# Two cross-attention layers on one core: where four loads, two stores and a split projection stand in each slot

## What is computed

```python
# layer 0 (8 heads of 40; the context's last 4 tokens are "ca", the first 73 "enc")
hs     = mha(x @ Wq, enc @ Wk, enc @ Wv)
ca_q1  = einsum('btc,th->bch', ca, Wq_ca)[:, indices]    # queries from 192 channels
ca_hs1 = mha(ca_q1, x, x)                                # keys and values are x itself
ca_hs2 = mha(ca_hs1 @ Wq, ca @ Wk_ca, ca @ Wv_ca)        # only 4 keys
x      = (hs + ca_hs2) @ Wout + b_out + x
# layer 1 (20 heads of 16, 77 keys)
out    = mha(x @ Wq1, ctx @ Wk1, ctx @ Wv1) @ Wo + bo + x
```

## Time and profile before

| what | value |
|---|---|
| runs | 377.20, 387.36, 387.67 us (median 387.36) |
| the profiled execution | 382.48 us; its span in the profile 380.6 us |
| mean granted clock of PE | 0.93 |
| PE busy (share of the span) | 331.5 us (87%) |
| PE weight loads, DVE, ACT, POOL busy | 257.9, 197.9, 161.1, 120.9 us |
| chain that ended last, by engine | PE 57%, ACT 11%, DMA 10%, DVE 9%, issue 6%, SP's queue 5% |
| DMA | 56.11 MB in 54468 packets, mean 147 GB/s |

### The profile page before, as it was taken

The page is one execution under the profiler, slowest core; times in us unless marked ns, Lnnn a source line. Parts: engine busy times, 40 slices in busy tenths (PEclk is TensorE's granted clock), DMA queues, the critical chain, the costliest instruction groups (busy, mean ns, idle before and its releaser), DMA issues.

```text
span 380.6 us, 7973 instructions
## 1 busy us (share of the span) xinstructions
PE 331.5 (87%) x3044; PEld 257.9 (68%) x3044; DVE 197.9 (52%) x431; ACT 161.1 (42%) x343; POOL 120.9 (32%) x124
## 2 busy tenths in 40 slices
PE   4998966999987999799979998999799979887685
PEld 2777654677755777687668767777687768646653
DVE  4552116272771478257736775377257742623544
ACT  3541550408451846074607461754084507350050
POOL 5836140025140714062306231714081203122201
PEclk9996998999985999799989999999699989979898
DMA  8998924704277527752685378628742872216011
GB/s 249 285 344 258 217 85 120 187 2 129 71 199 141 174 73 208 172 168 80 172 207 166 85 195 184 177 87 212 185 143 72 222 188 79 71 42 154 10 43 41
DMA packets 54468, 56.11 MB, mean 147 GB/s; under 512 B 17680, under 2 KB 47472, under 8 KB 54432
## 3 DMA queue, kind: packets, MB, share of 16 engines
q1 hardware_dynamic: 54432, 55.61, 53.6%
HBM read 36.12 MB, written 19.10 MB: 145 GB/s over the span
## 4 chain that ended last, share of the span: by engine, by line
PE 57%; ACT 11%; DMA 10%; DVE 9%; issue 6%; SPq 5%; POOL 1%; POOLq 0%; DVEq 0%; ACTq 0%
ACT prob L785 8%; PE bank L629 5%; DVE negm L910 5%; PE bank L452 4%; DMA q_scratch<-q 4%; PE bank L731 3%; PE bank L749 3%; PE bank L453 3%; PE bank L454 3%; PE bank L655 3%; PE bank L482 3%; PE bank L719 3%; PE bank L684 2%; PE bank L465 2%; PE bank L765 2%
## 5 line engine op out<-in xcount | busy, mean ns | idle before, releaser
L785 ACT ACTIVATE prob<-bank 77x512 f32<-77x512 f32 (+1 forms) x96 | 41.2, 529 | 22.6 <-PE bank L527 22.5
L910 DVE TENSOR_REDUCE negm<-bank 128x5 f32<-128x385 f32 (+2 forms) x88 | 42.5, 550 | 12.9 <-PE bank L765 12.9
L1167 POOL TENSOR_TENSOR at0lo<-atu,at0hi 120x512 fp32r<-120x512 f32 x8 | 14.8, 1854 | 107.1 <-ACT at0hi L775 107.1
L869 ACT ACTIVATE prob<-bank 73x512 f32<-73x512 f32 x32 | 16.3, 591 | 73.1 <-PE bank L713 73.1
L1175 POOL TENSOR_TENSOR xlo<-x,xhi 128x256 fp32r<-128x256 f32 x16 | 11.5, 738 | 77.1 <-DVE xhi L1056 77.1
L910 DVE TENSOR_REDUCE negmc<-bank 128x2 f32<-128x512 f32 x48 | 29.4, 681 | 7.8 <-PE bank L537 7.8
L525 PE MATMUL bank<-q,kp 32*77 32x256 f32 x320 | 24.9, 391 | 6.2 <-ACT prob L785 3.9
L684 PE MATMUL bank<-at0hi,wo 120*128 120x256 f32 x48 | 17.7, 370 | 13.8 <-issue 13.8
L775 ACT ACTIVATE q<-bank 120x512 fp32r<-120x512 f32 (+3 forms) x32 | 15.7, 489 | 27.9 <-PE bank L456 27.3
L1104 POOL TENSOR_TENSOR cast<-ca,small 96x1536 fp32r<-96x1536 f32 x8 | 22.3, 2790 | 13.1 <-PE bank L719 12.8
L876 ACT ACTIVATE prob<-bank 128x512 f32<-128x512 f32 x48 | 25.4, 624 | 0.0
(11 more groups left out here) (174 smaller groups left out, 866.1 us busy)
## 6 DMA issues: line engine op xcount, KB each, us to landing
q_scratch<-q SPq DMA_DIRECT2D x16, 360.0 KB, 4.2
q0s<-q_scratch SPq DMA_DIRECT2D x8, 640.0 KB
xt<-in_xt SPq DMA_DIRECT2D x8, 384.0 KB, 4.5
...
xkeys<-in_xkeys SPq DMA_DIRECT2D x8, 352.0 KB, 5.0
...
```

What stands on the lines that cost most here:

```text
L785: nc.scalar.activation(p1[:, h:h + n, :].rearrange("p h q -> p (h q)"), ps_of("SC1", j, d)[0:KEYS1, 0:n * SQ], ACT.Exp, scale=SCALE1)\
L869: nc.scalar.activation(p0[:, 2 * j:2 * j + 2, :].rearrange("p h q -> p (h q)"), ps_of("SC0", j, b)[0:KEYS0, :], ACT.Exp, scale=SCALE0)\
L910: return nc.vector.tensor_reduce(out=out, in_=in_, axis=AX, op=ALU.max, negate=True)
```

## The change

Four edits, with no change to the arithmetic.

- **SP.** The load of wo's rows stands first in the slot, ahead of denc. The channel keys (xkeys) are loaded after the two q0s loads instead of before them. The store of the output stands behind rb1's loads. In slot 8 rb1 is spread before atu1 is loaded. The denc of batch 0 is gathered at the end of slot 0.
- **OUT in two jobs.** In slots 3 to 7 OUT 1 (8 matmuls, and its addition on DVE) stands between CS and SC1 8; OUT 0 stays after S2. In slots 8 and 9 M1 stands between OUT 0 and OUT 1.
- **Setup.** V1 0-3 move ahead of CS in slot 1; CA stands ahead of V0 4-7 in slot 0. DVE's recc and atu0 of slot 1 stand behind the maxima.
- **Drain.** In slot 8 S2 and its exp stand ahead of all three PV1.

```diff
         if s4 and not s1:
-            jobs(e, "OUT", 0, 1)
+            jobs(e, "OUT", 0)
...
         if s3:
             jobs(d, "M1")
+        if s4 and not s1:
+            jobs(e, "OUT", 1)
...
+        if i == 1:
+            jobs(0, "V1", 0, 1, 2, 3)
...
             jobs(b, "CS", *range(6))
+        if s4 and s1:
+            jobs(e, "OUT", 1)
...
         if i == 0:
-            jobs(0, "V0", *range(3, B))
+            jobs(0, "V0", 3)
             jobs(0, "CA", 0, 1)
+            jobs(0, "V0", *range(4, B))
         if i == 1:
-            jobs(0, "V1", *range(B))
+            jobs(0, "V1", 4, 5, 6, 7)
+        if s2 and not s1:
+            jobs(c, "S2")
         if s3 and d < LAST:
-            jobs(d, "PV1", *(range(3) if s4 and s1 else range(1)))
+            jobs(d, "PV1", *(range(3) if s4 else range(1)))
...
-        if s2:
+        if s2 and s1:
             jobs(c, "S2")
         if s4 and s1:
-            jobs(e, "OUT", 0, 1)
-        elif s3 and d < LAST:
+            jobs(e, "OUT", 0)
+        elif s3 and not s4:
             jobs(d, "PV1", 1, 2)
...
                 if s2:
-                    drained(sp, "CU", c, 0, 1)
-                    sp.dma_start(denc[:, :], uc[D0:128:64, :, :]).then_inc(denc_in, 16)
+                    if c == 0:
+                        sp.wait_ge(v2w_st, 32)
+                    sp.dma_start(wo0[96:128, :, 2, :].bitcast(f32), v_d[c]).then_inc(v2w_in, 16)
+                    if c:
+                        gather_channel(c)
                     sp.wait_ge(recc_ready, c + 1)
...
                 if s1:
-                    if b:
-                        load_xkeys(b)
                     sp.wait_ge(q_st, 32 * (b + 1))
...
-                if s2:
-                    if c == 0:
-                        sp.wait_ge(v2w_st, 32)
-                    sp.dma_start(wo0[96:128, :, 2, :].bitcast(f32), v_d[c]).then_inc(v2w_in, 16)
+                    if b:
+                        load_xkeys(b)
...
-                if s4:
-                    store_out(e)
                 if s3 and d < LAST:
...
+                    if s1:
+                        load_rows1()
+                        spread_reciprocals1()
+                    else:
+                        spread_reciprocals1()
+                        load_rows1()
+                if s4:
+                    store_out(e)
...
+                    if b == 0:
+                        gather_channel(0)
...
                 if s4 and not s1:
-                    layer1_out(f)
-                if s2:
-                    dve.wait_ge(denc_in, 16 * (c + 1))
-                    nc.vector.reciprocal(recc[:, :], denc[:, :]).then_inc(recc_ready, 1)
...
+                    layer1_out(0)
+                if i > 1 and s2:
+                    channel_reciprocals()
+                if s4 and not s1:
+                    layer1_out(1)
+                if i > 1 and s2:
+                    layer0_rows()
                 if s1:
                     ca_maxima(*range(6))
+                if s4 and s1:
+                    layer1_out(1)
...
+                if i == 1:
+                    channel_reciprocals()
+                    layer0_rows()
                 if s2:
                     dve.wait_ge(rbc_in, 32 * (c + 1))
...
                 if s4 and s1:
-                    layer1_out(f)
+                    layer1_out(0)
```

138 lines of the change are left out of this document (81 added, 57 removed).

## The result

The changed kernel is **not faster, and in the first measurement slower**: 394.6 us in the median of 4 runs (387.8 to 398.3) against 385.1 for the kernel before (377.2 to 387.7), a ratio of 1.025 (95% interval 1.015 to 1.034). Run again later, it took 388.5 us (383.5 to 393.9, 4 runs) against 386.2, with no interval. A ratio in this text is taken over the runs within 1.5% of the fastest of their kernel, which are two of the four of the changed kernel each time, so it can stand up to 1% off the quotient of the medians. In the repetition these two (383.5 and 385.4) are level with the mean of the ten of the kernel before (384.6). So the kernel is between level and 2.5% slower, and whether it is slower by 2% is not settled. The forecast of 372 us and its range of 361 to 384 are missed by both medians, and no gain of any size was seen. The profiled executions took 392.3 and 383.5 us.

The account below looks back on a forecast made before the run. PE, busy 331.5 of 380.6 us, was taken as the bound, with SP's queue loop limiting the gain. From 382.5 us, -9.6 - 0.5 + 1 + 0 - 1.1 = -10.2 gave 372; own range 367 to 378, with two rivals 361 to 384.

Parts of the forecast that it names:

- wo first: Loading wo's rows first in the slot removes PE's stall ahead of O and its clock fall; 23.4 us at stake.
- A: Leg of SP's slot turn from line 424 to the load of q0s: 15.36 us in slot 3, to stay 15.4.
- C: Leg of SP's slot turn from rec1's start to the next line 424: 14.40 us in slot 3, to become 11.2.
- DVE path of 11.1 us: From rec1's start through rb1, the product, at1hi and rec0 to SP: 11.1 us, tying with C's 11.2.
- B: Leg of SP's slot turn from the load of q0s to rec1's start: 9.08 us in slot 3, to become 10.1.
- xkeys, "1.0" a slot: Loading xkeys behind q0s lengthens B by 1.0 us a slot, bounds -0.4 and 5.0.
- Rival 3: Slower (chance 0.08): xkeys ahead of the maxima and den1 cost B 5.0 us instead of 1.0; 395 to 400 us.
- The output store, "0.42 us of SP": Storing the output behind rb1 costs 0.42 us of SP ahead of xt and den0, within C.
- OUT in two, "0": OUT 1 moves to where PE waits for ACT's exps: 0, or -0.5 to +0.5 us a slot if PE decides.
- Setup, "0"; the bounds -1.5 and +1.5: Slots 0 and 1: V1's gain ahead of S2 is lost again behind late recc; 0 us, bounds -1.5 and +1.5.
- Drain, "-1.1": Slots 8 and 9: rb1 first and output last save about 0.8 us, M1 0.3 to 0.9; together -1.1 us.
- The two new waits, "+1, at most +8": PE waits at SC0 (about 1 us) and CU 1 (about 1.7); charged +1 us for all slots, at most +8.

Follow-up runs that it names:

- k0s early: W with k0s of the next batch loaded right behind xkeys instead of behind xt: 369.9 us, ratio 0.968.
- den0 early: W with the gather of den0 issued in front of xt and k0s instead of behind them: 386.7 us, ratio 1.007.
- W: The kernel before with wo's load first in the slot and OUT in two jobs, nothing else: 371.5 us (ratio 0.962), repeated 372.4 us (0.979).
- W + keys late: W with xkeys loaded behind q0s: 381.2 us, ratio 0.990.
- W with the whole setup: W with the setup work reordered as in the change: 379.4 us, ratio 0.984.
- recc early: W with the change's setup order, but slot 1's reciprocal of denc and product on atu0 ahead of the maxima: 365.1 us, ratio 0.950.
- W + drain: W with slots 8 and 9 reordered as in the change: 377.9 us, ratio 0.980.

## Why the prediction was wrong, step by step

**wo first: right in kind.** A stayed (15.0 against 15.4), O's stall went, and with it the fall of the clock there. Alone it gave 11.4 us in slots 2 to 7. By my terms it should have given more: -9.6 for six slots had 6 x 1.0 us for the keys already taken off. What is missing is in C.

**C, the step that failed.** I wrote that "both of SP's waits go: 14.40 - 3.1 - 0.5 + 0.4 = 11.2". It is 13.5 in slots 2 to 6, and 12.5 even with wo first alone. The waits did go; the leg did not get shorter by them. SP's timeline at the end of slot 3, before and changed (start us, us, queue, line, what):

```profile
164.02 0.34 SPq L303 DMA_DIRECT2D xt<-in_xt  x1
164.40 0.43 SPq L309 DMA_DIRECT2D k0s<-k_scratch  x1
164.87 0.45 SPq L311 DMA_DIRECT2D k0s<-k0lo_scratch  x1
168.50 0.55 SPq L414 DMA_DIRECT2D den<-u  x1
169.10 0.48 SPq L415 DMA_DIRECT2D u_scratch<-u  x1
169.62 0.42 SPq L416 DMA_DIRECT2D u0b_scratch<-u  x1
170.80 0.32 SPq L418 DMA_DIRECT2D rec_scratch<-rec  x1
```

```profile
166.47 0.34 SPq L416 DMA_DIRECT2D rec_scratch<-rec  x1
...
171.37 0.40 SPq L376 DMA_DIRECT2D out_t<-x  x1
171.88 0.36 SPq L312 DMA_DIRECT2D xt<-in_xt  x1
172.29 0.47 SPq L318 DMA_DIRECT2D k0s<-k_scratch  x1
172.81 0.67 SPq L320 DMA_DIRECT2D k0s<-k0lo_scratch  x1
173.58 0.55 SPq L436 DMA_DIRECT2D den<-u  x1
174.17 2.38 SPq L437 DMA_DIRECT2D u_scratch<-u  x1
176.59 0.43 SPq L438 DMA_DIRECT2D u0b_scratch<-u  x1
178.41 0.32 SPq L440 DMA_DIRECT2D rec_scratch<-rec  x1
179.40 0.81 SPq L448 DMA_DIRECT2D atu<-u_scratch  x2
```

The chain of waits names what is between the gather of den0 and its reciprocal, and DVE's rows (changed, slot 3) show it ahead of rec0:

```profile
173.58 4.53 DMA den<-u
```

```profile
174.54 0.96 DVE L1115 TENSOR_TENSOR atu<-atu,rb 128x768 f32<-128x768 f32 x1 [6.17 <-DMA rb<-rec_scratch]
175.53 0.56 DVE L1117 CAST at1hi<-atu 128x768 fp32r<-128x768 f32 x1
178.13 0.25 DVE L1133 RECIPROCAL rec<-den 128x16 f32<-128x16 f32 x1 [2.04 <-DMA den<-u]
```

Before, SP stood 3.1 us behind k0s' issue waiting for PV0. In that time most of the 657 KB of xt and k0s could leave the queue (xt lands 4.5 us behind its issue in the median, which is 168.5 here); the store of den0's reciprocal followed 2.30 us behind den0's issue (168.50 to 170.80). Without the wait den0 (8 KB) goes out 0.1 us behind k0s, behind xt, k0s and now the output store, and the same takes 4.83 us (173.58 to 178.41). So 2.5 of the 3.1 us come back as time behind the bulk. This recurs in slots 2 to 6 of the 17 profiles in which den0 stands behind xt and k0s, "k0s early" left out: 2.3 to 2.8 us where SP paused 2.5 us or more ahead of den0, 3.1 to 5.2 with a pause of 0.4 to 1.4, and 3.7 to 5.7 (4.8 in the mean) with one of 0.1. The store of u0 shows it too: 2.38 us to issue, 0.48 before. I had read SP's wait as plain loss; it was time in which the queue could empty. "k0s early" takes 273 KB from in front of den0, and is the one kernel in which C falls to 11.9; "den0 early" shows that the gather can't just be moved ahead.

My DVE path of 11.1 us agreed with 11.2 by luck, since it left out two terms. One is rec0's wait for den0: in slots 2 to 6 of the changed kernel rec0 stands for 1.9 to 2.2 us behind at1hi (0.6 to 2.7 in the repetition, 0.6 to 1.3 before). The other is the way from rec0's store to line 424, 1.0 us (178.41 to 179.40; before it was 170.80 to 171.97): C ends at line 424, and my path ended at the store. With rb1 0.5 us earlier than I had it, 11.1 + 2.0 + 1.0 - 0.5 = 13.6; slot 3's C is 13.4. A and B together came out 1.0 us a slot shorter than forecast, which hid part of the error. The Trainium skill ("DMA: Bandwidth & Descriptors", section Two DMAs through the same engine are not ordered) has it that descriptors of one queue of one DMA engine start in order; the trace agrees (4.83 us behind the bulk, 2.30 without), and I had weighed that rule for the keys alone.

**xkeys, "1.0" a slot: right.** B is 9.5 to 10.2 in all seven profiles with the keys late and 8.0 to 8.7 in the others; A is shorter by some 0.4, so a turn costs about 1.0 more. Slots 2 to 7 take 217.1 us in the mean of the seven profiles with wo first and neither DMA order changed (213.8 to 223.5, without "k0s early" and "den0 early"), 219.7 with only the store late (2 profiles), 223.1 with only the keys late (3; 220.6 to 225.5) and 225.1 with both (4; 223.2 to 226.8). That is 6.0 us for the keys, as my sum had it, and 2.0 to 2.6 for the store. The clock does not explain it: two of the three with the keys late stood at the lower level for only 7 us in these slots (220.6 and 225.5 us), W for 10 (214.3). In the medians the keys cost more, 8.8 us (W and W + keys late). The prediction's step holds; it was the change that gave 6 us away, since the keys cost at most the 0.4 us on A where they were. One of SP's two longest waits, and one that comes in every slot, is for q_scratch, the round trip of the queries, 23.6 us in 8 slots before:

```profile
SPq L368 <- DMA q_scratch<-q: 23.6, 8, 4.2
```

The keys stood directly ahead of that wait and went through the queue in it. Behind q0s they find the time to landing that the page of the changed kernel gives, 8.2 us instead of 5.0, and the maxima and den1 stand behind them:

```profile
xkeys<-in_xkeys SPq DMA_DIRECT2D x8, 352.0 KB, 8.2
```

Rival 3 named this mechanism, with the trigger "over 2.6 us on B". B rose by 0.8 in the changed kernel. So it did not come true as stated.

**The output store, "0.42 us of SP".** Alone it is 3 us in the medians, 2.0 to 2.6 in slots 2 to 7, both inside the scatter of W. Slot 7's C is 10.8 to 11.9 in the six profiles with the store late, and 9.8 to 10.6 in those with wo first and the store early, but for one (11.0). I counted the issue and left out its 384 KB in front of xt and den0.

**OUT in two, "0".** It gained 4 to 5 us in the medians (376.5 to 371.5 and 372.4), about 2 against each round's own kernel before, and C and A are not shorter. No gain is shown beyond the scatter, so "0" is not refuted.

**Setup, "0"; the bounds -1.5 and +1.5.** The path that I named ("recc now comes behind the maxima, and rbc, uc and S2 behind it") is the one that costs, and I let V1's gain cancel it. PE in slot 1: changed, W with the whole setup, and W with recc early (start us, us; in brackets the idle time before):

```profile
61.96 4.47 PE L506 MATMUL bank<-kp,u 96*77 96x320 f32 x16
68.33 4.47 PE L506 MATMUL bank<-kp,u 96*77 96x320 f32 x16
78.06 2.77 PE L582 MATMUL bank<-wk,uc 128*96 128x32 f32 x16 [4.93 <-DVE uc L1057]
80.64 9.09 PE L499 MATMUL bank<-u,q 96*128 96x308 f32 x24
```

```profile
76.31 2.77 PE L574 MATMUL bank<-wk,uc 128*96 128x32 f32 x16 [4.93 <-DVE uc L1044]
78.89 9.27 PE L491 MATMUL bank<-u,q 96*128 96x308 f32 x24
```

```profile
61.05 4.47 PE L498 MATMUL bank<-kp,u 96*77 96x320 f32 x16
68.71 4.53 PE L498 MATMUL bank<-kp,u 96*77 96x320 f32 x16 [0.15 <-DVE negmc L939]
73.41 1.51 PE L574 MATMUL bank<-wk,uc 128*96 128x32 f32 x16
74.76 6.47 PE L491 MATMUL bank<-u,q 96*128 96x308 f32 x24
```

4.93 us of waiting, then S2 at 2.77 instead of 1.51 and K1 at 9.1 to 9.3 instead of 6.47: 4.9 + 1.3 + 2.7 = 8.9 us on PE. V1 in two halves (2 x 4.47 instead of 10.5 to 12.3 in one piece) gives back 1.6 to 3.3, and PE no longer waits 1.4 to 3.6 us ahead of it. The balance, from the end of the queries to the end of K1: 27.5 to 29.1 us in the six profiles with the whole new order, 24.6 to 28.0 in the twelve with the old one (means 27.9 and 25.9), and 20.0 with recc early. So the new order cost about 2 us there, just beyond my bound, and the place of recc alone cost 7.8. PE sets the end of slot 1: in every profile but "den0 early" line 424 follows K1's end by 13.1 to 13.2 us. With recc late, q0 is also stored behind it, and A of slot 1 is 18.3 to 19.9 in the six profiles and 13.1 to 15.0 in the others; but since it is K1's end that line 424 follows, these 5 us are not what ends the turn. Slots 0 and 1 together take 97.6 to 102.9 us in those six, 94.4 to 104.1 in the twelve (means 100.8 and 97.8), and 94.4 with recc early, where slot 0 ends late (60.2) and slot 1's turn is the shortest of all (34.2).

**Drain, "-1.1".** The rest behind slot 7's line 424 takes 59.0 to 65.1 us in the seven profiles with the new order (mean 61.4) and 56.5 to 59.3 in the twelve without (mean 57.9): it costs some 3.5 us where I had -1.1. In these pieces PE stood at the lower clock for 22.6 us in the mean of the seven and for 15.1 in that of the twelve, and 7.5 us at half speed are 3.7 us of work; so the price may be that of the clock. S2 ahead of PV1 was "0"; PE waits there for uc while PV1 would be ready (W + drain):

```profile
331.38 2.77 PE L576 MATMUL bank<-wk,uc 128*96 128x32 f32 x16 [2.99 <-DVE uc L1045]
```

All seven have this wait, 2.7 to 3.4 us; of the others the longest is 0.2. From line 424 to den1's issue it is 20.3 us in their mean and 19.3 in the others: 1.0 of the 3.5. Spreading rb1 first depends on the store: from den1's issue to the product on atu1 it is 12.4 us before, 11.5 in the changed kernel (my 0.8 us, of which the store alone gives 0.3 to 0.6: 12.1 and 11.8 without the new order), and 13.2 to 13.6 with the store in front of rec1's. The other 2.5 us lie behind that product (28.7 against 26.2 in the means). In four of the seven the last 64 matmuls of slot 9's values took 6.6 to 7.1 us instead of 3.66, PE's clock being at 0.50 there in the changed kernel. Those four have the new setup order too, but so has the repetition of the changed kernel, where they took 3.66. What lowers the clock there is open.

**The two new waits, "+1, at most +8".** SC0's wait is 12.3 us, of which 3.5 in slots 2 to 7 (0.8, 0.5 and 2.2). The other 8.8 are in slot 0. There I had "CA earlier in slot 0 changes nothing": PE waits 4.3 to 8.8 us for the maxima's row in all seven profiles with the new setup order, and at most 3.4 in the others. This costs little, since SC0 then starts at 43.3 to 46.5 us in six of the seven and at 43.6 to 45.9 in the others with such a wait; 48.6 in the first profile of the changed kernel is scatter. The sign that I gave for a wrong forecast, a wait of over 2 us at SC0, came once in six slots, and the clock fell behind it.

## What to carry to other kernels

Before you price the removal of an engine's wait, ask what empties during it: a wait on an in-order DMA queue may be what makes the next small, urgent transfer quick. Bulk loads stood best here in front of a round trip that the queue waited for anyway, and not between it and the small rows that gate an engine. In a bundle of reorders that each look free, run the parts alone: here two parts gave the forecast's number, on other legs than forecast, and the place of one reciprocal of 0.2 us and the product behind it was worth 7.8 us on PE in slot 1 and 14 us in the medians. When you end a path at a store, add what stands between it and the next turn.

## What the runs showed of the chip

- The granted clock against idle time, in windows of PE (us, busy, clock, DMA share, GB/s). Changed kernel, slot 1: V1's first half, the wait for uc, S2, K1.

```profile
61.96:66.40 4.44, 4.44 (x20) 1.00 0.36 110
73.10:78.06 4.96, 0.03 (x1) 0.76 0.67 204
78.06:80.80 2.74, 2.74 (x17) 0.50 0.34 62
80.90:89.60 8.70, 8.70 (x24) 0.71 0.66 138
```

  The clock fell to its lower level (0.50 is 1.2 GHz) in a wait of 4.9 us and stayed there through S2 and part of K1. The stalls of 0.81 and 0.54 us at SC0 in slots 3 and 4 had no such fall behind them. The one of 2.17 us in slot 6 had: 1.00 in it, and 0.50 from 281 us on, with PE busy throughout.

```profile
276.00:278.60 2.60, 0.43 (x5) 1.00 0.79 206
281.00:283.00 2.00, 2.00 (x6) 0.50 0.61 192
```

- V1 in one piece of 32 matmuls ran at a mean clock of 0.72 in W (12.2 us, busy throughout); cut into two halves, each ran at 1.00 in the changed kernel. W's V1 has no wait in it, but a wait just ahead of it, in which the clock fell:

```profile
65.01 0.70 PE L639 MATMUL bank<-kbd,q 80*128 80x146 f32 x2 [2.45 <-DVE negmc L930]
```

```profile
64.00:65.70 1.70, 0.69 (x3) 0.50 0.09 8
65.70:77.90 12.20, 12.20 (x35) 0.72 0.74 195
```

  All twelve profiles with the old setup order have this wait (1.4 to 3.6 us) and a V1 of 10.5 to 12.3 us, where two halves at 1.00 take 8.9. With V1 0-3 ahead of CS the wait is gone, or 0.7 us with recc early.
- SP's own time to issue one store of 384 KB was 0.48 us before, 3.8 us behind the issue of xt and k0s, and 2.38 us in the changed kernel, 0.7 us behind it. In "k0s early", with 273 KB less in front of it, it was 0.46 to 0.73 us in slots 2 to 6.
